# A two-layer cross-attention kernel on one core: start-up order rearranged, two-tile score lead in the first layer, all hardware loops written out

## What is computed

```python
# layer 0: 16 heads of 32, hidden size 2048
x = x + attention(layer_norm(x), ctx, mask) @ cproj_w + cproj_b
x = x + gelu_tanh(layer_norm(x) @ fc_w + fc_b) @ proj_w + proj_b
# layer 1: twice (a = 0, 1) an attention with 16 heads of 128 and one
# learned extra key and value, then one perceptron of hidden size 2048
for a in (0, 1):
    x = x + attention_a(layer_norm(x), ctx, extra_key, extra_value) @ wo + bo
x = x + gelu(layer_norm(x) @ w_fc1 + b_fc1) @ w_fc2 + b_fc2
```

## Time and profile before

| | |
|---|---|
| median of 3 runs | 2390.0 us (2389.43 to 2390.95) |
| the profiled execution, its own time | 2393.2 us |
| its span in the trace | 2391.3 us |
| busy: PE / PE weight loads / DVE / ACT / POOL | 97% / 88% / 56% / 48% / 16% |
| mean granted TensorE clock | 0.995 of full speed |
| moved by DMA | 376 MB, 157 GB/s |

### The profile page before, as it was taken

The page is one execution under the profiler, slowest core; times in us unless marked ns, Lnnn a source line. Parts: engine busy times, 40 slices in busy tenths (PEclk is TensorE's granted clock), DMA queues, the critical chain, the costliest instruction groups (busy, mean ns, idle before and its releaser), DMA issues.

```text
span 2391.3 us, 45273 instructions
## 1 busy us (share of the span) xinstructions
PE 2313.3 (97%) x13859; PEld 2103.7 (88%) x13859; DVE 1342.9 (56%) x3154; ACT 1146.4 (48%) x2531; POOL 376.4 (16%) x739
## 2 busy tenths in 40 slices
PE   6899899999999999999999999999999999999999
PEld 5677678888999998999998788999998999998888
DVE  5677774443556555565554514555565555554743
ACT  4677752354445544445453444454444455453421
POOL 4011126430000100100101120001001001002421
PEclk9999989999999999999999999999999999999999
DMA  5322126474455645645635464455545546544110
GB/s 167 123 77 84 61 80 220 176 238 138 162 184 184 192 172 183 206 170 181 225 129 169 174 180 130 167 186 188 202 163 179 206 162 211 193 137 153 58 54 31
DMA packets 232451, 376.32 MB, mean 157 GB/s; under 512 B 57278, under 2 KB 185682, under 8 KB 232258
## 3 DMA queue, kind: packets, MB, share of 16 engines
q1 hardware_dynamic: 232258, 373.87, 47.0%
HBM read 315.77 MB, written 58.05 MB: 156 GB/s over the span
## 4 chain that ended last, share of the span: by engine, by line
PE 90%; DVE 3%; issue 3%; ACT 3%; DMA 0%; ACTq 0%; SPq 0%; DVEq 0%
PE ps_k L1508 10%; PE ps_k L1509 9%; PE ps_k L1510 9%; PE ps_o L1508 9%; PE ps_o L1510 8%; PE ps_o L1509 8%; PE ps_v L1508 6%; PE ps_v L1509 6%; PE ps_v L1510 6%; PE ps_s L1508 4%; PE ps_s L1510 4%; PE ps_s L1509 4%; PE ps_t L1667 3%; PE ps_t L1607 1%; PE ps_o L1619 1%
## 5 line engine op out<-in xcount | busy, mean ns | idle before, releaser
L1508 PE MATMUL ps_k<-cs_hi,w_a_hi 128*128 128x376 f32 x1152 | 391.7, 340 | 7.0 <-DVE k_lo L1284 4.3
L1509 PE MATMUL ps_k<-cs_lo,w_a_hi 128*128 128x376 f32 x1152 | 385.4, 335 | 0.0
L1510 PE MATMUL ps_k<-cs_hi,w_a_lo 128*128 128x376 f32 x1152 | 384.2, 333 | 0.0
L986 ACT ACTIVATE prob<-ps_s,row_columns 112x376 f32<-112x376 f32 x256 | 147.2, 575 | 300.3 <-DVE row_columns L1290 300.3
L767 POOL CAST k_hi<-xk_hi 128x1 fp32r x256 | 47.0, 184 | 1274.4 <-PE ps_s L1510 1274.4
L1508 PEld LDWEIGHTS ps_k<-cs_hi,w_a_hi 128*128 128x128 f32 x1152 | 217.3, 189 | 12.6 <-DVE k_lo L1284 8.8
L1509 PEld LDWEIGHTS ps_k<-cs_lo,w_a_hi 128*128 128x128 f32 x1152 | 217.5, 189 | 0.1
L1510 PEld LDWEIGHTS ps_k<-cs_hi,w_a_lo 128*128 128x128 f32 x1152 | 217.0, 188 | 0.0
L1284 DVE SCALAR_TENSOR_TENSOR k_lo<-ps_k,col_b,k_hi 128x375 fp32r<-128x375 f32 x256 | 155.2, 606 | 99.3 <-ACT k_hi L954 94.7
L954 ACT ACTIVATE k_hi<-ps_k,col_b 128x375 fp32r<-128x375 f32 x256 | 146.3, 572 | 102.2 <-PE ps_k L1510 99.3
L731 POOL TENSOR_TENSOR w_b_lo<-w_raw_b,w_b_hi 128x512 fp32r<-128x512 f32 x88 | 120.0, 1391 | 420.4 <-ACT w_b_hi L817 420.3
(11 more groups left out here) (256 smaller groups left out, 5964.0 us busy)
## 6 DMA issues: line engine op xcount, KB each, us to landing
ckd_hi<-context_by_key_halves SPq DMA_DIRECT2D x64, 768.0 KB, 4.3
ckd_lo<-context_by_key_halves SPq DMA_DIRECT2D x64, 768.0 KB, 5.8
cs_hi<-context_halves SPq DMA_DIRECT2D x64, 752.0 KB, 5.9
cs_lo<-context_halves SPq DMA_DIRECT2D x64, 752.0 KB, 7.3
w_raw_b<-in_blocks_b SPq DMA_DIRECT2D x104, 256.0 KB, 3.9
w_raw_a<-in_blocks_a SPq DMA_DIRECT2D x104, 256.0 KB, 4.6
q<-q_scratch SPq DMA_DIRECT2D x72, 224.0 KB, 5.7
shared<-extra_probability SPq DMA_DIRECT2D x32, 448.0 KB, 4.6
```

The lines of the kernel that those rows point to most:

```text
L986: act.activation(prob[buf][0:LQ, 0:KW], ps_s[buf][0:LQ, 0:KW], ACT.Exp, bias=max_neg[0:LQ, buf:buf + 1], accum_out=prob_sum[0:LQ, buf:buf ...
L1508: pe.matmul(out, w_h, m_h, start=first, stop=False)
L1509: pe.matmul(out, w_h, m_l, start=False, stop=False)
L1510: return pe.matmul(out, w_l, m_h, start=False, stop=last)
```

## The change

- SP loads context 0 first, then the four pieces of the value weights, then the five constants, rows 0 to 3 of x, the query weights, rows 4 to 6 of x, context 1, the mask.
- ACT runs one square root at the very start on a constant, and no longer waits for the column constants before `schedule`. It splits the value weights before any deviation, the query weights in two halves around rows.
- DVE splits context 0 and the lo parts of both first weight blocks itself (POOL no longer does) and writes the column constants between them; only then does it take x, two row tiles at a time.
- PE runs the first value product before any row, the second between rows 1 and 2, and rows 4, 5, 6 are turned after query products 0, 1, 2. The staging buffers of queries 2 and 3 are exchanged (in every query stage), with their waits one row apart.
- In `attend_first` the scores of tile t+2 are issued before `weighted` of tile t; before, the scores of tile t+1 were issued at the head of tile t. In its prologue the first key tile is read out before the queries are split.
- In the last block of the first perceptron ACT scales rows 0 and 1 before it splits the next query weights, rows 2 to 4 after it.
- All `Fori` loops are Python loops, so every iteration is written out.

```diff
-            with eng.Fori(1, 3) as fg:
+            for fg in range(1, 3):
                 mlp(0, fg, 1, RT * (fg + 1))
             mlp(0, 3, 1, RT * 4, norm=2)
-            with eng.Fori(0, 2) as a:
+            for a in range(0, 2):
...
-            with eng.Fori(1, PAIRS - 1) as p:
+            for p in range(1, PAIRS - 1):
                 pair_of(ATT0, 0, 0, p, one_batch)
...
-                with eng.Fori(1, PAIRS - 1) as p:
+                for p in range(1, PAIRS - 1):
                     pair_of(ATT1, a, group, p, one_batch)
...
-            with eng.Fori(1, GROUPS - 1) as group:
+            for group in range(1, GROUPS - 1):
                 block(group)
...
-            return (prob[0], prob[1], o[0], o[1])[i][:, 0:HALF]
+            return (prob[0], prob[1], o[1], o[0])[i][:, 0:HALF]
...
+            if isinstance(norm, int) and norm == 0:
+                return {0: (4,), 1: (5,), 2: (6,)}
             return {0: (5,), 1: (6,)}
...
+            load_context(Place(ATT0, 0, 0, 0, 0))
+            load_first_block(1)
             sp.dma_start(ident[:], eye).then_inc(vecs_in, 16)
...
             load_x(0)
-            load_context(Place(ATT0, 0, 0, 0, 0))
-            load_first_block(1)
+            load_first_block(0)
             load_x(1)
-            load_first_block(0)
...
-            split_lo(1, 0)
-            split_lo(0, 0)
             pool.wait_ge(vec_split, 2)
...
                 if isinstance(e, int) and e == 0:
+                    split_hi(1, 0, range(4), None)
                     deviation(0, 0)
                     deviation(0, 1)
+                    split_hi(0, 0, (0, 1), None)
+                    deviation(0, 2)
+                    deviation(0, 3)
+                    value_out(Place(ATT0, 0, 0, 0, 0), 0)
+                    act.wait_ge(vec_ev, 4)
                     scaled(0, 0)
-                    deviation(0, 2)
                     scaled(0, 1)
-                    split_hi(1, 0, range(4), None)
-                    deviation(0, 3)
+                    split_hi(0, 0, (2, 3), None)
+                    value_out(Place(ATT0, 0, 0, 0, 0), 1)
                     scaled(0, 2)
                     scaled(0, 3)
-                    split_hi(0, 0, range(4), None)
                     deviation(0, 4)
-                    value_out(Place(ATT0, 0, 0, 0, 0), 0)
                     deviation(0, 5)
-                    value_out(Place(ATT0, 0, 0, 0, 0), 1)
-                    scaled(0, 4)
-                    deviation(0, 6)
...
-                        act.wait_ge(ln_lo, RT * norm + RT)
+                        act.wait_ge(ln_lo, RT * norm + RT + i - 3)
...
                 def prologue(place):
+                    key_hi(place, 0)
                     split_q(place)
-                    key_hi(place, 0)
...
-                for r in range(3 if norm is not None else 0):
-                    deviation(norm, r)
+                if norm is not None:
+                    for r in range(3):
+                        deviation(norm, r)
+                    scaled(norm, 0)
+                    scaled(norm, 1)
+                    deviation(norm, 3)
                 split_hi(0, na + 1, range(4), lambda s: (h_mm, HIDDEN * (4 * m + fg) + HIDDEN - 4 + s + 1))
...
-            act.wait_ge(vec_ev, 4)
+            act.wait_ge(cleared, 1)
+            act.activation(std[:, 0:1], eps_column[:, 0:1], ACT.Sqrt).then_inc(warm, 1)
...
+                    context_hi(first)
+                    first_context_lo(first)
+                    split_lo(1, 0, range(4))
+                    columns()
+                    dve.wait_ge(x_in_sem[0], 16)
+                    measure_rows((0, 1))
+                    scale_rows((0, 1))
+                    measure_rows((2, 3))
+                    scale_rows((2, 3))
+                    halves(0, 0)
+                    halves(0, 1)
+                    split_lo(0, 0, range(4))
+                    halves(0, 2)
+                    halves(0, 3)
+                    dve.wait_ge(x_in_sem[1], 16)
+                    measure_rows((4, 5))
+                    scale_rows((4, 5))
+                    measure_rows((6,))
+                    halves(0, 4)
+                    scale_rows((6,))
+                    halves(0, 5)
+                    halves(0, 6)
...
-                    for r in range(4):
-                        turn_row(0, r)
-                    for i in range(2):
-                        value(Place(ATT0, 0, 0, 0, 0), i)
-                    turn_row(0, 4)
+                    first = Place(ATT0, 0, 0, 0, 0)
+                    value(first, 0)
+                    turn_row(0, 0)
+                    turn_row(0, 1)
+                    value(first, 1)
+                    turn_row(0, 2)
+                    turn_row(0, 3)
...
                     score_quad(place, 0)
                     value(place.next(), 0)
+                    score_quad(place, 1)
...
                     for t in range(NT):
-                        if place.key(t + 1):
-                            score_quad(*place.key(t + 1))
                         for j in range(SUB0):
                             turn(place, t, j)
...
+                        if place.key(t + 2):
+                            score_quad(*place.key(t + 2))
                         weighted(place, t)
```

More of the change, by code:

```diff
@@ L248, in build @@
         vec_t, vec_ev, vec_split, xv_diff = (sem(n) for n in ("vec_t", "vec_ev", "vec_split", "xv_diff"))
-        cleared = sem("cleared")
+        cleared, warm = sem("cleared"), sem("warm")
         w_in = [sem(f"w_in_{s}") for s in "ab"]
@@ L712, in load_first_block @@
                     sp.dma_start(w_raw[slot][:, c, :], src[:, c, :]).then_inc(w_in[slot], 16)
-            load_x(0)
             load_context(Place(ATT0, 0, 0, 0, 0))
             load_first_block(1)
+            sp.dma_start(ident[:], eye).then_inc(vecs_in, 16)
+            sp.dma_start(prob[0][0:N_CA, 0:P], vec_a).then_inc(vecs_in, 16)
+            sp.dma_start(prob[0][:, P:2 * P], vec_b).then_inc(vecs_in, 16)
+            sp.dma_start(prob[0][0:32, 2 * P:3 * P], value_rows).then_inc(vecs_in, 16)
+            sp.dma_start(prob[0][0:32, 3 * P:4 * P], value_bias_rows).then_inc(vecs_in, 16)
+            load_x(0)
+            load_first_block(0)
             load_x(1)
-            load_first_block(0)
             load_context(Place(ATT0, 0, 0, 0, 1))
@@ L821, in deviation @@
                 act.wait_ge(ln_agg, RT * e + r + 1)
+                if isinstance(e, int) and (e, r) == (0, 0):
+                    act.wait_ge(warm, 1)
                 act.sem_inc(act_waited, 1)
@@ L872, in query @@
                         scaled(norm, row)
+                    if not layer and i == 0:
+                        deviation(0, 6)
                     if norm is not None and layer and i == 3:
@@ L1096, in mlp @@
                     split_hi(1, nb + 1, range(4), lambda s: (y_mm, x0 + RT))
-                for r in (3, 4) if norm is not None else ():
-                    deviation(norm, r)
-                    for row in TURNS_LATE[r]:
+                if norm is not None:
+                    deviation(norm, 4)
+                    for row in (2, 3, 4):
                         scaled(norm, row)
-                if norm is not None:
-                    scaled(norm, 3)
-                    scaled(norm, 4)
                     deviation(norm, 5)
                     deviation(norm, 6)
-            act.wait_ge(vec_ev, 4)
+            act.wait_ge(cleared, 1)
+            act.activation(std[:, 0:1], eps_column[:, 0:1], ACT.Sqrt).then_inc(warm, 1)
             schedule(act, ln, skip, query, attend_first, attend, project, mlp)
@@ L1149, in ln @@
                     first = Place(ATT0, 0, 0, 0, 0)
-                    for r in range(RT):
-                        if r:
-                            reciprocal_deviation(0, r - 1)
-                        if r == 4:
-                            normalized(0, 3)
-                            halves(0, 2)
-                        for i, (r0, _) in enumerate(X_PARTS):
-                            if r == r0:
-                                dve.wait_ge(x_in_sem[i], 16)
-                        statistics(0, r)
-                        if r and r != 4:
-                            normalized(0, r - 1)
-                        mean_variance(0, r)
-                        if r == 2:
-                            context_hi(first)
-                        if r in (2, 3, 5):
-                            halves(0, r - 2)
-                        if r == 3:
-                            first_context_lo(first)
@@ L1169, in ln, with scale_rows, measure_rows @@
-                    reciprocal_deviation(0, RT - 1)
-                    normalized(0, RT - 1)
-                    for r in (4, 5, 6):
-                        halves(0, r)
+                    def scale_rows(rows):
+                        for r in rows:
+                            reciprocal_deviation(0, r)
+                            normalized(0, r)
```

(7 more changed lines are left out.)

42 lines of the change are left out of this document (19 added, 23 removed).

## The result

The kernel after takes **2387.69 us** (median of 20 runs, 2384.66 to 2390.68) against 2391.07 us of the kernel before (20 runs): ratio 0.9983, 95% interval 0.9976 to 0.9989, so 3.4 us less. The forecast was 2370, the range 2359 to 2381. The direction came true, the size did not: by the prediction's own line of 4.8 us this is no change, to which it gave 0.05. The profiled execution took 2384.85 us, 2.8 less than its median, the one of before 2.1 more than its own: the two traces differ by 8.2 us of span, and 3.4 of it is the change.

A forecast was written before the change was run, and what follows sets the result against it. It took PE's gaps, chiefly at loop jumps and in the start, as the bound. −18.5 − 6.1 + 6 − 1 = −19.6 us took the profiled 2393.2 to 2373.6, with the median 3.2 lower: 2370, range 2359 to 2381.

The forecast's parts named there:

- Loops written out: Jumps of the group loop and the loop over a: removing PE's stops there saves 18.5 us, bounds 13.6 to 20.
- no "issue": Sign of being right: PE shows no "issue" gap over 1 us after 350 us.
- price of 0 for the pair and perceptron loops: Pair loops and the perceptron's loop: no gap on PE seen there, so writing them out wins 0.
- Scores before the weighted sum: First layer's attention: later weighted sums delay ACT's and DVE's queues, +6 us, bounds −3 and +12.
- Start: First norm and projections: queries start and end earlier, 6.1 us saved in total, bounds 4 to 8.5.
- timetable: Start of the kernel: first value product at 12.6, queries from 27.1, second half at 41.3, end at 51.1 us.
- exchange of staging buffers: Query stages: it loosens a wait PE never felt, 0; if felt, at most 0.64 us.
- Norm behind the first perceptron: ACT scales rows ahead of the weight split, where PE waited 1.27 us: −1 us, bounds −2.5 and +1.5.
- free exchange: Rival on the score order: delays in ACT's and DVE's queues are slack, so 2364 us; chance 0.22.
- jumps cost little: Rival on the loops: gaps come from transfers at the same places and stay, 2388 us; chance 0.04.
- late code: Rival on written-out code: late instruction fetches stop PE, 2401 us with 12 stops; chance 0.04.
- The start wins little: Rival on the start: queries' second half waits for row 6, only 1 to 2 us won, 2375 us; chance 0.12.

The follow-up runs named there:

- e1: The kernel before with every hardware loop written out and nothing else: 2375.59 us, ratio 0.9934.
- e12: The kernel before with only the group loop and the loop over a written out, loops over pairs and thirds kept: 2377.11 us.
- e2: The kernel after with the old order of scores, start and loops as changed: 2374.59 us, ratio 0.9930.
- e5: The kernel after, but at t = 2 the next scores stand behind the weighted sum as before: 2379.65 us.
- e6: The kernel after, but at t = 1 the next scores stand behind the weighted sum as before: 2379.39 us.
- e9: The kernel of e2 with ACT's work behind the first perceptron in its old order, weight split ahead of the first scaled rows: 2373.71 us.
- e10: The kernel of e2 with row 6 of the first norm scaled ahead of ACT's read-out of query product 2: 2375.07 us.
- e13: The kernel of e9 with unused identity turns on PE, 26 before the first query product and 14 before the second scores: 2369.22 us.
- e4: The kernel before with the scores of tile t+2 put ahead of the weighted sum of tile t, nothing else: 2406.80 us, ratio 1.0066.
- e3: The kernel after with all hardware loops put back, start and score order as changed: 2410.73 us, ratio 1.0087.

## Why the prediction was wrong

- **Loops written out, −18.5: right in kind, 2.8 too much.** The marks came as forecast: groups 173.9 apart, no "issue". e1 measures 15.7 us, within the bounds of 13.6 to 20. In the traces the group loop gave back 3.5 and 5.9 of 3.7 and 6.1, the stretch from 1273.73 to 1594.83 (the jump of a in it) 8.0 where 9.2 was taken. Part of the 93.5 against 86.6 us was a lower clock (0.97 in before at 1320 to 1380 us, 1.00 in after). The price of 0 for the pair and perceptron loops was 1 to 2 us too low (e12). The marks 583.16 and 1456.63, called the first key read-out, are the fourth in both blocks, so their difference stands.
- **Scores before the weighted sum, +6: the step that failed.** The worked sum was right: +1.3 a batch, 9 over seven, and the traces of after and e2 show 1.35 (31.74 less 30.39), 9.5 over seven, and 10.9 from the first scores to the last weighted sum. It fell with the words "where PE's own fill bounds a tile the delay is absorbed", which, with a tenth of a microsecond back in each other tile, took it down to 6 without a row. Nothing was absorbed. The split was off too: 0.5 at t = 1 and 0.9 at t = 2 were foreseen, e5 and e6 give 0.7 each, a score quad's length. In the median the exchange costs 13.1, beyond the upper bound of 12. The spans of the two traces differ by 9.9; the other 3.2 are that after's profiled run lay 2.8 us below its median and e2's 0.4 above.
- **Start, −6.1: about −2 (e9 against e1; 2.8 by the first weighted sum in the traces).** Two terms failed. First, the timetable: the queries began at 28.2, not 27.1 (ACT's chain ended at 26.7, not 26, and row 2's halves stood behind DVE's own weight split until 25.9), and the second half at 43.4, not 41.3. The prediction gave the exchange of staging buffers a price of 0, "it loosens one wait that PE never felt". But it was the new timetable that had to be checked: the third read-out is staged in the buffer of row 5 and waits 1.59 us for its halves, with row 6 behind it on ACT; e10 wins 0.5 of this. Second, the clock: "behind an idle PE of some 4 us, so I give it 4.4 instead of 2.5 us" saw the slow first product (4.65) and not the second fall at 68 to 70 us, which costs 1.4 us by e13's first weighted sum. With 2.2 us of timetable and 1.4 of clock the 6.1 come down to 2.5.
- **Norm behind the first perceptron, −1: 0 or worse** (e9: +0.9 for having it, ranges overlap). The 1.27 us went, but a wait of 2.71 us for DVE took their place, which the prediction had nowhere. From the last weighted sum to the second block's first read-out it is 251.0 us in e1, 251.2 in e2 and 249.7 in e9.
- **Sum.** The three terms off: loops +2.8, start and norm +6.1 (7.1 forecast, 1.0 by e2 and e1), exchange +7.1: 16.0 us. The kernel lies 17.7 above the forecast; 1.1 of the rest is the median of before, 2391.07 over 20 runs and 2390.0 over the first three. That the kernel still came out faster rests on the loops, which hid an exchange twice as dear as forecast.
- **Rivals.** The free exchange was refuted by e2, "jumps cost little" by e1 (its own terms give 2389, not 2388; the time measured is near it for another reason), and late code by the trace: PE has no "issue" of 1 us after 350 us. "The start wins little" happened, together with an exchange at its upper bound; no case joined the two, and so the range ended at 2381. In the trace the batch came out at 31.7, where 32 was said to show the forecast right: the sign was there, but its price had been cut. The longest tile lies between the weighted sums of t = 1 and t = 2.

## What to carry to other kernels

When a worked sum from rows says 9, a cut to 6 for "what may be absorbed" needs its own row: look whether the engines on the path wait for each other in turn, for then each microsecond put on it counts in full. Moving work ahead of an engine's wait is only worth it if what the wait protects is late; here the scores came early and stood ready while DVE's queue waited. And where PE must idle for some microseconds between products, look at the granted clock behind the wait, and try idle turns in it: 40 and 26 of them were worth more here than the whole reordering of the start. Last, a part's worth depends on what else is there: time each in both orders, as the 1.0 us gain and the 3.9 us loss of the same start and norm show.

## What the runs showed of the hardware

- The granted clock fell behind a wait of 2.48 us in after, e2, e9 and e4, and not behind a wait of the same 2.48 us in before and e1: the length of one wait does not tell it alone. Behind the wait of 4.59 us it fell in after, e2 and e9 alike.
- At the very start the first product's matmuls follow each other at 0.43 us, all twelve before (26.39 on) and the first eight after (13.04 on), and then at 0.23, while the windows show a granted clock of 1.00. The prediction called this pace the lower level of the clock. The windows can't show it, as the record of the clock begins just where the pace changes (31.4 us in before, 16.9 in after); but later 512-column matmuls follow each other at 0.43 us where the clock is recorded as 0.50 (before, 313 us).
- A hardware loop costs more than its jump where PE is not full: 0.3 us in each batch in the old order, 0.7 in the new one (e3), against none that shows in the second layer's pairs (a group of 173.9 us with its pair loop, e12, and 173.8 to 174.2 without, e1). What in the loop makes it was not tried.
- A 1024 KB transfer that landed in 5.7 us behind the small constants took 8.2 us behind the context, four weight pieces and the constants; DVE waited only 0.59 us for it.
